# Unpadded queries and keys with scores in four row groups, and a new order around them, in a graph-attention and soft-routing kernel

## The reference

```python
z = layernorm(x)
q, k, v = z @ wq + bq, z @ wk + bk, z @ wv + bv        # split into 8 heads of 48
attn = softmax(q @ k.T * 48**-0.5 + adj)
r = rmsnorm(z + (attn @ v) @ wo + bo, alpha1, gamma1)
y = rmsnorm(r + silu(r @ w1 + b1) @ w2 + b2, alpha2, gamma2)
x = x + y
```

## Time and profile before

| | before |
|---|---|
| median of 3 runs | 3154.0 us (3153.85 to 3154.65) |
| profiled execution | 3154.54 us, span 3152.7 us, mean granted clock 0.972 |
| PE busy | 2925.6 us (93%) |
| DVE, ACT, POOL busy | 60%, 49%, 47% |
| setup until the first groups | 0 to 54 us |
| layer 1 | about 54 to 1870 us |
| dispatch | about 1870 to 2235 us |
| experts | about 2235 to 3060 us |
| combine, first load to the end | 3066.0 to 3152.7 us |

### The profile page before, as it was taken

How to read it: one execution, slowest core, us unless ns; L and a number is a source line. 1 busy time by engine, 2 the same in 40 slices (tenths; PEclk the granted TensorE clock), 3 DMA queues, 4 the chain that set the end, 5 groups by cost and what they waited for, 6 DMA issues and landing times. The chain is left out here.

```text
span 3152.7 us, 62729 instructions
## 1 busy us (share of the span) xinstructions
PE 2925.6 (93%) x21523; PEld 2822.0 (90%) x21523; DVE 1877.5 (60%) x3053; ACT 1535.9 (49%) x3982; POOL 1472.6 (47%) x1486
## 2 busy tenths in 40 slices
PE   3999999999999999999999857788799999999986
PEld 2999999999999999999999847788799999999982
DVE  4465656565665656565665525555577777777754
ACT  3354554545454554545454425555545545544530
POOL 0344444343444444343444424444377677677650
PEclk9899999999999999999999968899899999999999
DMA  4010101010010101010110133432566666666869
GB/s 127 13 41 25 45 25 45 25 45 23 33 36 25 45 25 45 25 45 23 35 35 25 34 95 115 120 118 75 176 210 208 209 210 213 205 212 205 265 224 367
DMA packets 289913, 320.82 MB, mean 102 GB/s; under 512 B 23688, under 2 KB 289416, under 8 KB 289800
## 3 DMA queue, kind: packets, MB, share of 16 engines
q1 hardware_dynamic: 281128, 307.17, 31.2%
q10 hardware_dynamic: 8704, 12.58, 1.1%
HBM read 260.97 MB, written 58.72 MB: 101 GB/s over the span
## 5 line engine op out<-in xcount | busy, mean ns | idle before, releaser
L1531 PE MATMUL u_bank<-x_in,x_w 128*128 128x256 f32 x4608 | 574.5, 283 | 5.7 <-DVE x_w L1619 5.7
L1531 PEld LDWEIGHTS u_bank<-x_in,x_w 128*128 128x128 f32 x4608 | 569.6, 192 | 5.8 <-issue 5.8
L927 POOL TENSOR_TENSOR hT_lo<-h_tmp,hT_hi 128x512 fp32r<-128x512 f32 x192 | 248.0, 1292 | 432.0 <-DVE hT_hi L815 432.0
L1688 POOL TENSOR_TENSOR x_aT<-x_act,x_aT 128x512 fp32r<-128x512 f32 x128 | 299.6, 2341 | 182.1 <-ACT x_aT L1596 182.1
L388 PE MATMUL m_bank<-yT_hi,w_hi 128*128 128x256 f32 x1152 | 339.7, 295 | 0.0
L388 PE MATMUL m_bank<-yT_lo,w_hi 128*128 128x256 f32 x1152 | 324.4, 282 | 0.0
L388 PE MATMUL m_bank<-yT_hi,w_lo 128*128 128x256 f32 x1152 | 323.7, 281 | 0.0
L1684 POOL TENSOR_TENSOR x_w<-raw,x_w 128x768 fp32r<-128x768 f32 x128 | 274.2, 2142 | 102.4 <-DVE x_w L1627 102.4
L661 ACT ACTIVATE h_tmp<-m_bank,b1c 128x256 f32<-128x256 f32 x384 | 160.9, 470 | 329.8 <-PE m_bank L388 329.4
L1587 ACT ACTIVATE x_gelu<-u_bank,x_b1T 128x256 f32<-128x256 f32 x256 | 121.9, 476 | 409.8 <-PE u_bank L1531 409.8
L1543 PE MATMUL o_bank<-x_w,x_aT 128*128 128x384 f32 x1536 | 287.8, 335 | 1.8 <-POOL x_aT L1688 1.8
(11 more groups left out here) (214 smaller groups left out, 7307.6 us busy)
## 6 DMA issues: line engine op xcount, KB each, us to landing
raw<-in_L_ffn_w_dram SPq DMA_DIRECT2D x384, 384.0 KB, 4.7
ws_raw<-in_L_ffn_w_slot_dram SPq DMA_DIRECT2D x32, 576.0 KB, 5.0
x_in<-in_x_dram SPq DMA_DIRECT2D x32, 384.0 KB, 3.4
x_res<-in_x_dram SPq DMA_DIRECT2D x32, 384.0 KB, 4.1
residual<-f_sb SPq DMA_DIRECT2D x32, 384.0 KB, 2.5
yn<-yn_sb SPq DMA_DIRECT2D x32, 384.0 KB, 2.5
expert_out<-x_o SPq DMA_DIRECT2D x64, 192.0 KB, 3.0
c_o<-expert_out SPq DMA_DIRECT2D x32, 384.0 KB, 5.8
```

Source lines behind the costliest of these rows:

```text
L927: nc.gpsimd.tensor_tensor(hT[i % 3][1][:], h_tmp[i % 2][:], hT[i % 3][0][:].bitcast(F32), ALU.subtract).then_inc(hl.sem, 1)
L1531: mm = pe.matmul(u_bank[n % BANKS][:, g, :], w1s[i % 2][a][:, c, g, c2 * P:(c2 + 1) * P], xT[e % 2][b][:, c, :], start=c == 0 and j == 0, ...
L1688: nc.gpsimd.tensor_tensor(aTs[i % 2][1][:], aT[i % 2][:], aTs[i % 2][0][:].bitcast(F32), ALU.subtract).then_inc(al.sem, 1)
```

## The change

Five things change.

1. **Queries and keys are not padded.** `wq` and `wk` are kept with 384 columns, arranged so that each head's first 32 dimensions stand in one of two slices (four heads a slice, 32 rows each), and the last 16 dimensions of all heads in a third. Q and K are three slices instead of four. The third slice of the queries is written twice, each time scaled by a column with zeros for one half of the heads (`half_scale`, `half_bias`).
2. **Scores in four row groups.** A head's scores are two products of 32 rows, accumulated in PSUM: its own 32 dimensions, then the shared slice with the masked queries. A tile's 8 heads are 16 products in four row groups and four banks (the three `a_bank` and what was `r_bank`). Both tiles' scores stand next to each other. The new waits ahead of them are for both `v_sb` (`v_ok` 2) and for the routing's last use of the fourth bank; `xnT_step` waits for all four adds of the scores on DVE (`sc_ok` 4), since it writes into the same bank.
3. **A new order in the layer's body**, on PE, ACT and DVE. `down` 0 and 1 stand behind the scores, `up` 2 behind PT 0, and ACT does all 16 exponentials before the routing's copies.
4. **Dispatch.** `load_ws(t, 1)` moves forward in SP's queue, and ACT's `ws_high(t, 1)` behind two `turn`s.
5. **Experts and combine.** The buffers `raw1` and `raw2` become one tile `raw`. When the last expert has read its pieces, `combT` (kept in DRAM as slot by tile) is loaded into it, in five DMAs, and the last 8 residual groups behind the others in `slots2T`; the stores of experts 30 and 31 are issued after these. The combine loads `o` alone, and its loop is written out.

In the setup, the clearing of the padded stages goes, `wq` and `wk` come by one DMA each, their split is in three pieces each, and `bq` and `bk` come by 32 small DMAs instead of 16.

Cut to its core, the diff is:

```diff
-    U_Q, U_K, U_V, U_S = (0, 1), (2, 3), (4, 5), ((6, 7), (8, 9))
-    U_PT, U_CTX, U_CT, U_WO, U_YT = ((10, 11), (13, 14)), (12, 16), (15, 18), (17, 19), (20, 21)
-    A_BANK = [a_bank[u % 3] for u in range(20)] + [a_bank[0], a_bank[2]]
-    ZT_BANK = [a_bank[2], a_bank[1]]
+    U_Q, U_K, U_V, U_S = (0, 1), (2, 3), (4, 5), (6, 7)
+    U_PT, U_CTX, U_CT, U_WO, U_YT = ((8, 9), (11, 12)), (10, 14), (13, 16), (15, 17), (18, 19)
+    A_BANK = [a_bank[i] for i in (0, 1, 2, 0, 1, 2)] + [None, None] + [a_bank[i] for i in (0, 1, 2, 0, 1, 2, 0, 1, 2, 0, 2, 1)]
...
-                for half in range(2):
-                    m = 2 * n + half
-                    mm = split_mm(bank[:, half * GN:(half + 1) * GN],
+                for m in ((0, 1), (2,))[n]:
+                    mm = split_mm(bank[:, (m % 2) * GN:(m % 2 + 1) * GN],
                                   [[w[s][:, c, tok(m)] for s in range(2)] for c in range(DC)],
                                   [[zT[s][:, c, :] for s in range(2)] for c in range(DC)])
                 mm.then_inc(a_full.sem, 1)
...
-            def scores(g, t):
-                pe.wait_ge(q_ok.sem, q_ok.at(g, 4))
-                pe.wait_ge(k_ok.sem, k_ok.at(g, 4))
-                for par in range(2):
-                    held, k = ((k_ok, 4), (v_ok, 1), (v_ok, 2), (sc_ok, 1))[2 * t + par]
-                    pe.wait_ge(held.sem, held.at(g, k))
-                for m in range(H // 2):
-                    for par in range(2):
-                        r = slice(HP * par, HP * par + DH)
-                        mm = pe.matmul(A_BANK[U_S[t][par]][:, tok(m)], qT[r, m, tok(t)], kT[r, m, tok(t)], start=True, stop=True)
-                        if m == H // 2 - 1:
-                            mm.then_inc(a_full.sem, 1)
+            def scores(g, t, r):
+                if t == 0:
+                    pe.wait_ge(q_ok.sem, q_ok.at(g, 4))
+                    pe.wait_ge(k_ok.sem, k_ok.at(g, 3))
+                    pe.wait_ge(v_ok.sem, v_ok.at(g, 2))
+                    if r is not None and past(r, 1):
+                        pe.wait_ge(sl_ok.sem, sl_ok.at(r - 1, 2))
+                for m in range(2):
+                    for q, k in ((m, m), (2 + m, 2)):
+                        for i in range(4):
+                            rows = slice(HG * i, HG * i + HG)
+                            mm = pe.matmul(banks[:, i, t * GN + m * P:t * GN + (m + 1) * P], qT[rows, q, tok(t)],
+                                           kT[rows, k, tok(t)], start=k < 2, stop=k == 2)
+                mm.then_inc(a_full.sem, 1)
...
-            def xnT_step(g, t):
+            def xnT_step(g, t, a):
                 pe.wait_ge(xn_ok.sem, xn_ok.at(g, t + 1))
                 if t == 0:
-                    if past(g, 1):
+                    if a is not None:
+                        pe.wait_ge(sc_ok.sem, sc_ok.at(a, 4))
+                    elif past(g, 1):
...
+                if A: project(a, U_Q, wq_s, 0)
                 if M: up(m, 0)
-                if A: project(a, U_K, wk_s, 0); project(a, U_K, wk_s, 1)
+                if A: project(a, U_Q, wq_s, 1); project(a, U_K, wk_s, 0)
                 if M: up(m, 1)
-                if A: values(a, 0); values(a, 1); scores(a, 0)
-                if R: xnT_step(r, 0)
-                if M: down(m, 0)
-                if A: scores(a, 1)
-                if R: xnT_step(r, 1)
+                if A: project(a, U_K, wk_s, 1); values(a, 0); values(a, 1); scores(a, 0, r); scores(a, 1, r)
+                if M: down(m, 0); down(m, 1)
+                if R: xnT_step(r, 0, a)
                 if A: prob_T(a, 0)
+                if M: up(m, 2)
+                if A: context(a, 0); prob_T(a, 1)
+                if R: xnT_step(r, 1, a)
+                if M: up(m, 3)
                 if R: logits(r)
-                if A: context(a, 0)
-                if M: down(m, 1)
-                if A: prob_T(a, 1)
                 if R: logits_T(r)
-                if M: up(m, 2)
-                if A: context_T(a, 0); context(a, 1)
-                if M: up(m, 3)
-                if A: project_out(a, 0); context_T(a, 1)
+                if A: context_T(a, 0); context(a, 1); project_out(a, 0); context_T(a, 1)
...
             def query(g, half):
-                for m in (2 * half, 2 * half + 1):
-                    if m % 2 == 0:
-                        act.wait_ge(a_full.sem, a_full.at(g, U_Q[m // 2] + 1))
-                    bank = A_BANK[U_Q[m // 2]]
-                    nc.scalar.activation(qT[:, m, :], bank[:, (m % 2) * GN:(m % 2 + 1) * GN], ACT.Identity,
-                                         bias=bqk[:, 0, m:m + 1], scale=DH ** -0.5).then_inc(q_ok.sem, 1)
+                act.wait_ge(a_full.sem, a_full.at(g, U_Q[half] + 1))
+                bank = A_BANK[U_Q[half]]
+                for m in range(2):
+                    if half:
+                        nc.scalar.activation(qT[:, 2 + m, :], bank[:, 0:GN], ACT.Identity, bias=half_bias[:, m:m + 1],
+                                             scale=half_scale[:, m:m + 1]).then_inc(q_ok.sem, 1)
+                    else:
+                        nc.scalar.activation(qT[:, m, :], bank[:, m * GN:(m + 1) * GN], ACT.Identity,
+                                             bias=bqk[:, 0, m:m + 1], scale=DH ** -0.5).then_inc(q_ok.sem, 1)
...
-                if A: query(a, 0); query(a, 1)
+                if A: query(a, 0)
                 if M: silu(m, 0)
+                if A: query(a, 1)
                 if R: square(r, 0, "z", z2_ok, xn, zms, zss); square(r, 1, "z", z2_ok, xn, zms, zss)
                 if M: silu(m, 1)
                 if A: nc.scalar.activation(warm[:, 0:1], nhalf[:, 0:1], ACT.Exp)
+                if A: exps(a, 0); exps(a, 1)
                 if R: xnT_step(r, 0)
-                if A: exps(a, 0)
+                if A: prob_T(a, 0)
                 if R: xnT_step(r, 1)
-                if A: prob_T(a, 0); exps(a, 1)
+                if A: prob_T(a, 1)
                 if R: logits(r); comb_exp(r)
-                if A: prob_T(a, 1)
+                if A: hi_T(a, 0, U_CT, cT[0][:], ch)
...
                     dve.wait_ge(adj_landed.sem, adj_landed.at(g, 16))
+                dve.wait_ge(a_full.sem, a_full.at(g, U_S[1] + 1))
                 for par in range(2):
-                    dve.wait_ge(a_full.sem, a_full.at(g, U_S[t][par] + 1))
-                    nc.vector.tensor_tensor(s_sb[t][:, par, :, :], A_BANK[U_S[t][par]][:].rearrange("p (m n) -> p m n", n=P),
-                                            adj_sb[:, t, :].unsqueeze(1).broadcast_to([P, H // 2, P]), ALU.add).then_inc(sc_ok.sem, 1)
+                    pair = banks[:, 2 * par:2 * par + 2, t * GN:(t + 1) * GN].rearrange("p b (m n) -> p b m n", n=P)
+                    nc.vector.tensor_tensor(s_sb[t][:, par, :, :].rearrange("p (b m) n -> p b m n", b=2), pair,
+                                            adj_sb[:, t, :].unsqueeze(1).unsqueeze(1).broadcast_to([P, 2, 2, P]), ALU.add
+                                            ).then_inc(sc_ok.sem, 1)
...
@@ -1082,10 +1104,10 @@
                 if O: store_ct(d, 0)
                 if T and R: load_ws(t, 0)
                 if O and T and t < E1 - 1: load_yn(t + 1, 0, 1, 2, 3)
+                if T and R: load_ws(t, 1)
                 if O and R: load_cb(d + 1, 1)
                 if O: store_ct(d, 1)
                 if O and T and t < E1 - 1: load_yn(t + 1, 4, 5, 6, 7)
-                if T and R: load_ws(t, 1)
...
-                means(t, 0); turn(t, 4); turn(t, 5); ws_high(t, 1); turn(t, 6); turn(t, 7)
+                means(t, 0); turn(t, 4); turn(t, 5); turn(t, 6); turn(t, 7); ws_high(t, 1)
...
+            ct_of = ct_dram.rearrange("p b n -> p (b n)")
+            n_ct = NB * P
+            for i in range(PIECES):
+                sp.wait_ge(w1_lo.sem, w1_lo.at(NX - 1, i + 1))
+                sp.dma_start(raw[:, i * RAW1:(i + 1) * RAW1], ct_of[:, i * RAW1:(i + 1) * RAW1]).then_inc(ct_landed.sem, 16)
+                if i == 1:
+                    sp.wait_ge(xl.sem, xl.at(NX - 1, 1))
+                    sp.dma_start(early[:, EARLY:NB, :], res_dram[EARLY * P:NB * P, :].rearrange("(g p) d -> p g d", p=P)
+                                 ).then_inc(res_landed.sem, 16)
+            sp.wait_ge(w2_lo.sem, w2_lo.at(NX - 1, PIECES))
+            sp.dma_start(raw[:, PIECES * RAW1:n_ct], ct_of[:, PIECES * RAW1:n_ct]).then_inc(ct_landed.sem, 16)
```

209 lines of the change are left out of this document (105 added, 104 removed).

## The result

The changed kernel takes 3182.9 us (median of 4 runs, 3180.8 to 3185.2), against 3153.9 for the kernel before in the same comparison: a ratio of 1.0094, 95% interval 1.0079 to 1.0109. It is slower, where 3133 us had been forecast. The profiled execution has a span of 3183.4 us.

A forecast was written before the change was run, and what follows sets the result against it. PE was taken to bound the layer, ACT's wait for a load to slow the dispatch, and DMAs to pace the combine. Layer +36, dispatch -46, combine -15, setup +4: 3154 became 3133 us, range 3075 to 3190.

The forecast's parts named there:

- The experts change at nothing: Experts' loop: same instructions on the same operands, so a change of 0 us.
- t = 16.52 us: Layer body: time from the first Q product to the start of the last score pair, 16.52 us.
- rival B: Layer's scores: only two score records run at a time, +53 us, 3186 us, slower; chance 0.17.
- Forecast 0.56, 0.52, 0.7 and 1.5: Layer body: PE's waits in us before `xnT_step`, CTX 0, the logits' transposes (LT) and `down` 5.
- 55.7: Layer: steady body's period in us against 54.52, +1.2 a body, +36 us over 30 bodies.
- ±3: Layer's first and last bodies: a change within 3 us either way.
- Rival C: Layer: waits behind the scores don't come; 3081 us with half gone, 3028 with all; chance 0.17.
- The floor of 52.2 us a body: Layer: body's period if none of the waits behind the score burst came, -69 us for the layer's term.
- Dispatch (-46: Dispatch: earlier load and ACT's new order each remove the wait for `w_slot2`; -46 us, range -33 to -51.
- combine (-15: Combine: runs at the DMAs' rate and moves 5.7 MB less at 389 GB/s; -15 us, from -10 to -19.
- Rival D: Dispatch keeps its wait, for a buffer or the DMAs: -5 in place of -46, 3174 us, slower; chance 0.10.
- The setup's +4: Setup: 16 more small DMAs on SP against fewer other issues and no clearing wait; +4 us, -1 to +9.

The follow-up runs named there:

- two moves: Changed kernel with 80 more PE instructions, plus `up` 1 between values and scores and the attention's bias ahead of a split on POOL: 3095.3 us, 0.9811.
- a third: The two moves plus, on ACT, tile 1's last four exponentials behind the copies of tile 0's transposed probabilities: 3073.2 us, ratio 0.9739 to the kernel before.

## Why the prediction was wrong

The direction was wrong, by one step in the first place. **"The experts change at nothing: the same instructions on the same operands; the chain there is PE's."** Each part of the sentence is true and the conclusion isn't: the experts lost 40.8 us to instruction packets, because the new layer has 105 PE instructions more in front of the loop (9410 against 9305) and the loop's code came to lie over one block more. With 45 or 80 instructions added, the change is 0.2% faster than before. That would have been the forecast direction, but 7 us in place of 21: the layer, below, is the rest.

**The layer's first part, t = 16.52 us, was right** to 0.1: 18 products less, the wait for `v_sb` (0.85, forecast 0.82), four records at a time. The last was in doubt, and rival B hung on it. The Trainium skill's rule of strict order (TensorE: Matmul & The Clock Gate, Part 3) would have needed 33 slots of 0.112, 3.7 us; the burst took 2.00, as its row above shows. The measured time, 3183, is within 3 us of B's 3186 and is not B: that it fell into the stated range is luck.

**The waits behind it were right in place, and the chain to the last of them was summed too short.** Forecast 0.56, 0.52, 0.7 and 1.5, measured 0.43, 0.30, 0.46 and 1.0, with 0.32 for WO 0, which the forecast hadn't. The brackets leave out the start-up beside a wait. Counted from start to start, against the same products without a wait in the same body, CTX 0's costs 0.48 (`up` 2 takes 2.68, `up` 3 2.20) and `down` 5's 1.45 (the two products ahead of it hold PE 1.80, the same kind 0.35 earlier in the body), near the forecast. Still `down` 5, which POOL releases, starts 0.6 us later than forecast. What the sum had too small is the piece from t to POOL's fourth split, 22.5 us by the forecast, 23.0 in the trace (1092.83, and t is 1053.28 + 16.5). DVE and POOL there, of after:

```profile
1090.67 0.42 DVE L839 CAST hT_hi<-h_tmp 128x512 fp32r<-128x512 f32 x1
1091.29 1.46 DVE L839 CAST hT_hi<-h_tmp 128x512 fp32r<-128x512 f32 x1 [0.19 <-ACT h_tmp L683]
```
```profile
1091.17 1.29 POOL L949 TENSOR_TENSOR hT_lo<-h_tmp,hT_hi 128x512 fp32r<-128x512 f32 x1 [13.26 <-DVE hT_hi L839]
1092.83 1.27 POOL L949 TENSOR_TENSOR hT_lo<-h_tmp,hT_hi 128x512 fp32r<-128x512 f32 x1 [0.36 <-DVE hT_hi L839]
```

A cast of 0.42 us took 1.46 beside POOL's split, and ends 0.3 us after it. I had summed it at 0.43: that is 1.0 us more, and the rest of the piece came out 0.5 shorter. The Trainium skill (SBUF — State Buffer, "Who interferes with whom") has DVE and GpSimd share a pair of ports under an exclusive lock; the row agrees, but no run here moved the cast away from POOL, so this part is read and not tested. From that split to `down` 5 it was 14.36 us (1107.19 - 1092.83), forecast 14.3. A body of 56.1 in place of 55.7 is 12 us of the 19; the rest is in the bodies at both ends, which I had at ±3: the first, which has no feed-forward, went from 43.6 to 46.7 us, and the end from the last group's Q to the dispatch from 131.4 to 137.7. Why was not tested.

**Rival C's reason fell as well**: the waits do come. But its thought that they are not the machine's limit was right: 52 us of them went with two moves, and 23 with a third. The floor of 52.2 us a body was not reached; the shortest was 53.87.

**Dispatch (-46, measured -48.7) and combine (-15, measured -16.8) were right** in place and size. In the dispatch "the two edits take the wait away twice over" holds only for one of them: the earlier load alone keeps the whole gain, ACT's order alone half. Rival D is refuted by this. **The setup's +4 was +0.1**: 16 more small loads and what went away cancel; no run took them apart.
